# Attention heads' outputs transposed by VectorE in squares of 32 and placed through DRAM; row moments of layers 0 and 2 by ScalarE in two passes

## The reference, cut to what matters

```
h   = layernorm(x)                       # the input of layers 0 and 2
# one layer:
q, k, v = split(shift_token(h) @ wqkv)   # 8 heads of 64
q, k = rotary(l2norm(q)), rotary(l2norm(k))
o   = softmax(q k^T + window mask) v     # windows of 64, looking one window back
x   = h + o @ wo
x   = x + gated MLP(layernorm(shift_token(x)))
```

## Time and profile before

| | us |
|---|---|
| median of 3 runs | 3070.74 (3067.27 to 3071.34) |
| profiled execution | 3069.8 |
| its span, first to last instruction | 3068.0 |
| PE busy | 2989.9 (97%) |
| DVE busy | 2589.6 (84%) |
| ACT busy | 2090.5 (68%) |
| POOL busy | 1746.9 (57%) |

### The profile page before, as it was taken

The page is one execution under the profiler, slowest core; times in us unless marked ns, Lnnn a source line. Parts: engine busy times, 40 slices in busy tenths (PEclk is TensorE's granted clock), DMA queues, the critical chain, the costliest instruction groups (busy, mean ns, idle before and its releaser), DMA issues.

```text
span 3068.0 us, 84550 instructions
## 1 busy us (share of the span) xinstructions
PE 2989.9 (97%) x30773; PEld 2157.2 (70%) x30773; DVE 2589.6 (84%) x5526; ACT 2090.5 (68%) x5016; POOL 1746.9 (57%) x1158
## 2 busy tenths in 40 slices
PE   7999999999999999989999699999999999999999
PEld 4777777667777777657777477777766677777765
DVE  7999998678888888869999599999966888888866
ACT  4777777437777777328889377777753677777732
POOL 8888886125666665540000588888721566666610
PEclk8999999999999999999999799999999999999999
DMA  5222222202222232100000122222320122222221
GB/s 131 50 51 51 50 59 60 48 16 48 49 52 50 51 65 57 41 1 1 1 1 1 24 52 50 53 50 52 70 48 19 42 49 53 50 49 59 57 49 42
DMA packets 311515, 138.26 MB, mean 45 GB/s; under 512 B 225897, under 2 KB 276546, under 8 KB 311106
## 3 DMA queue, kind: packets, MB, share of 16 engines
q1 hardware_dynamic: 311106, 132.84, 19.8%
HBM read 28.13 MB, written 19.66 MB: 16 GB/s over the span
## 4 chain that ended last, share of the span: by engine, by line
PE 90%; DVE 4%; issue 2%; POOL 2%; ACT 1%; SPq 0%; DMA 0%; DVEq 0%; ACTq 0%; POOLq 0%
PE psum L1264 14%; PE psum L1139 11%; PE psum L1238 7%; PE psum L1281 7%; PE psum L1312 7%; PE psum L1292 7%; PE psum L1194 6%; PE psum L1165 5%; PE psum L1226 5%; PE psum L1522 3%; PE psum L1326 3%; PE psum L1339 3%; PE psum L1498 3%; PE psum L1184 3%; PE psum L1508 2%
## 5 line engine op out<-in xcount | busy, mean ns | idle before, releaser
L491 POOL TENSOR_TENSOR rnorm<-ssq_floor,neg_half 128x16 f32<-128x16 f32 x256 | 750.4, 2931 | 499.7 <-DVE qkr L813 494.9
L566 ACT ACTIVATE shared<-psum,neg_max 128x128 f32<-128x128 f32 x2048 | 595.2, 396 | 40.5 <-DVE neg_max L789 40.5
L496 POOL TENSOR_TENSOR qk_cos<-qk_cos,qk_sin 128x1024 f32<-128x1024 f32 x256 | 607.3, 2372 | 0.0
L1264 PE MATMUL psum<-wqkv,hT 128*128 128x512 f32 x1024 | 533.6, 605 | 15.2 <-DVE qk_sin L775 8.5
L587 ACT COPY shared<-psum 128x512 f32<-128x512 f32 x256 | 150.1, 586 | 438.2 <-PE psum L1226 438.2
L775 DVE TENSOR_TENSOR qk_sin<-psum,sin 128x512 f32<-128x512 f32 x512 | 350.5, 685 | 101.8 <-ACT sq L573 100.9
L780 DVE TENSOR_TENSOR qk_cos<-psum,cos 128x512 f32<-128x512 f32 x512 | 350.6, 685 | 80.0 <-ACT sq L573 79.8
L625 ACT ACTIVATE shared<-psum,b1g 128x512 f32<-128x512 f32 (+1 forms) x192 | 131.6, 686 | 353.8 <-PE psum L1139 350.7
L573 ACT ACTIVATE sq<-psum 128x512 f32<-128x512 f32 x512 | 334.2, 653 | 25.3 <-PE psum L1264 25.3
L1139 PE MATMUL psum<-shared,w1g 128*128 128x512 f32 (+1 forms) x768 | 345.6, 593 | 5.4 <-DVE shared L879 4.0
L1292 PEld LDWEIGHTS psum<-wo,shared 128*128 128x128 f32 x2048 | 267.6, 191 | 115.6 <-issue 114.9
(11 more groups left out here) (132 smaller groups left out, 6373.5 us busy)
## 6 DMA issues: line engine op xcount, KB each, us to landing
vprev<-v SPq DMA_DIRECT2D x512, 130.0 KB, 2.3
token_blocks<-blocks SPq DMA_DIRECT2D x236, 64.0 KB, 1.6
hT<-token_blocks SPq DMA_DIRECT2D x944, 16.0 KB, 1.8
shared<-Y SPq DMA_DIRECT2D x32, 256.0 KB
shared<-Y SPq DMA_DIRECT2D x32, 224.0 KB
out<-X SPq DMA_DIRECT2D x8, 512.0 KB, 3.2
X<-in_L_attn_x SPq DMA_DIRECT2D x7, 512.0 KB, 6.7
wqkv<-in_L_ffn_wqkv SPq DMA_DIRECT2D x4, 512.0 KB, 3.6
```

The source lines that it names most:

```text
L491: nc.gpsimd.tensor_tensor(rnorm[:], ssq_floor[:], neg_half[:], ALU.pow).then_inc(rnorm_ready, 1)
L496: nc.gpsimd.tensor_tensor(both, both, qk_sin[:, t.m % 2, :], ALU.add).then_inc(sum_ready, 1)
L566: last = nc.scalar.activation(probs[:, c * P:(c + 1) * P], bank(3 + i, (c % 4) * P, (c % 4 + 1) * P), ACT.Exp, bias=neg_max[:, c:c + 1])
L1264: nc.tensor.matmul(bank(i), hT[:, t.m * P:(t.m + 1) * P], wqkv[:, i * INNER:(i + 1) * INNER], start=True, stop=True).then_inc(qk_psum, 1)
```

## The change

The heads' outputs of tiles 0 to 57 of each layer no longer go through PE. DVE transposes o in place squares of 32 (`heads_blocks`), SP stores the squares to DRAM in 4 DMAs and loads them back transposed in 4 more, and `project_out` reads them. The last 6 tiles keep the old way. DVE's maxima, sums and shares are joined to one instruction each, with the weighted values in PSUM banks 6 and 7 and not 7 and 2. The moments of the pairs of rows in layers 0 and 2 leave DVE: ACT sums a row while copying it (`row_sums`, slot s), POOL makes minus the mean (`row_means`, slot s), ACT sums the squares of row minus mean (`row_squares`, slot s+1), and POOL takes the root and normalises (`normalise_pair`, slot s+1).

```diff
+LAST = 6
...
+        def by_dma(t):
+            return t.row < NT - LAST
+        def act_units(L, s):
+            if L % DEPTH == 0 and s % 2 == 0 and 0 <= s and s + 14 < NT:
+                return range(s + 14, s + 16)
 # SP
+            def store_heads(t):
+                k = dma_count(t)
+                sp.wait_ge(head_blocks_ready, k + 1)
+                wait(sp, heads_in[k % 2], 64 * (k // 2))
+                squares = heads_out[k % 2].rearrange("x i n -> i x n")
+                for b in range(P // SQUARE):
+                    sp.dma_start(squares[:, :, b * SQUARE:(b + 1) * SQUARE],
+                                 head_blocks[b * SQUARE:(b + 1) * SQUARE, k % 2, :]...).then_inc(heads_stored[k % 2], 16)
+            def load_heads(t):
+                sp.wait_ge(heads_stored[k % 2], 64 * (k // 2 + 1))
+                wait(sp, attn_ready, before(t, 2))
+                for j in range(P // SQUARE):
+                    sp.dma_start(o_T[j * SQUARE:(j + 1) * SQUARE, k % 2, :]..., squares[j]).then_inc(heads_in[k % 2], 16)
...
+                if (t := tile_at(L, s - 1)) and by_dma(t):
+                    store_heads(t)
                 if t := tile_at(L, s + 3):
...
+                if (t := tile_at(L, s - 1)) and by_dma(t):
+                    load_heads(t)
 # POOL
+            def row_means(L, s):
+                pool.wait_ge(sum_of_row, p + 1)
...
+                nc.gpsimd.tensor_scalar(row_sum[:, 2:4], row_sum[:, 0:2], -1.0 / P, None,
+                                        ALU.mult).then_inc(mean_of_row, 1)
             def local_slot(L, s):
                 if t := tile_at(L, s + 4):
                     root(t)
                     total(t)
...
+                if act_units(L, s):
+                    row_means(L, s)
+                if rows := act_units(L, s - 1):
+                    normalise_pair(L, s - 1, rows)
 # ACT
+            def row_squares(L, s, rows):
+                act.wait_ge(mean_of_row, p + 1)
+                wait(act, eps_of_row, p)
+                for i, row in enumerate(rows):
+                    last = nc.scalar.activation(Y[:, row, :], X[:, row, :], ACT.Square, bias=row_sum[:, 2 + i:3 + i],
+                                                accum_out=row_sum[:, 4 + i:5 + i])
...
                 if t := tile_at(L, s + 4):
                     squares(t, 1)
+                if rows := act_units(L, s):
+                    row_sums(L, s, rows)
+                if rows := act_units(L, s - 1):
+                    row_squares(L, s - 1, rows)
                 if t := tile_at(L, s):
                     weights(t, 0)
```

More of the change, by code:

```diff
@@ L568, in exponents, with row_sums @@
                 last.then_inc(probs_ready, 1)
+            def row_sums(L, s, rows):
+                if L == 0:
+                    act.wait_ge(loaded[rows[0] // MT], 16)
+                else:
+                    act.wait_ge(x_ready, rows[-1] + 1)
+                wait(act, mean_of_row, pair_count(L, s))
+                for i, row in enumerate(rows):
+                    last = nc.scalar.activation(Y[:, row, :], X[:, row, :], ACT.Copy, accum_out=row_sum[:, i:i + 1])
+                last.then_inc(sum_of_row, 1)
+            def row_squares(L, s, rows):
+                p = pair_count(L, s)
+                act.wait_ge(mean_of_row, p + 1)
+                wait(act, eps_of_row, p)
+                for i, row in enumerate(rows):
+                    last = nc.scalar.activation(Y[:, row, :], X[:, row, :], ACT.Square, bias=row_sum[:, 2 + i:3 + i],
+                                                accum_out=row_sum[:, 4 + i:5 + i])
+                last.then_inc(squares_of_row, 1)
             def squares(t, i):
@@ L584, in outputs @@
             def outputs(t):
-                wait(act, oT_psum, before(t, 0))
+                act.wait_ge(oT_psum, last_count(t) + 1)
                 wait(act, attn_ready, before(t, 1))
@@ L784, in maxima @@
             def maxima(t):
[L785 to L790 removed]
+                scored = psum[:, 3 * BANK:5 * BANK].rearrange("p (h k) -> p h k", k=P)
@@ new lines, in heads_blocks @@
+            def heads_blocks(t):
+                k = dma_count(t)
+                dve.wait_ge(o_ready, t.n + 1)
+                wait(dve, heads_stored[k % 2], 64 * (k // 2))
+                if t.row == 0 and t.L == DEPTH:
+                    dve.wait_ge(out_psum, NT)
+                elif t.row == 0:
+                    wait(dve, mlp_ready, NG * t.L)
+                nc.vector.transpose(head_blocks[:, k % 2, :].rearrange("p (j c n) -> p j c n", j=4, c=4),
+                                    o.rearrange("p (c j n) -> p j c n", c=4, j=4)).then_inc(head_blocks_ready, 1)
@@ L1218, in heads_transpose @@
             def heads_transpose(t):
-                wait(pe, o_ready, before(t, 0, 2))
+                wait(pe, o_ready, before(t, 0))
                 if u := tile_at(t.L, t.row + 3):
@@ L1231, in weigh_values @@
                 pe.wait_ge(vprev_ready[t.m % 4], 32 * (t.n // 4 + 1))
-                wait(pe, o_ready, before(t, 1, 2))
+                wait(pe, o_ready, before(t, 1))
                 pe.wait_ge(probsT_ready, 2 * t.n + 2)
@@ L1272, in project_v @@
                     wait(pe, rot_ready, 4 * (t.n + 1) + 2)
-                elif u := tile_at(t.L, t.row - 5):
-                    wait(pe, oT_ready, before(u, 0))
+                elif u := tile_at(t.L, t.row - 2):
+                    wait(pe, qT_ready, before(u, 0))
                 else:
@@ L1284, in project_out @@
             def project_out(t):
-                wait(pe, oT_ready, before(t, 0))
+                if by_dma(t):
+                    k = dma_count(t)
+                    pe.wait_ge(heads_in[k % 2], 64 * (k // 2 + 1))
+                    squares = o_T[:, k % 2, :].rearrange("p (c n) -> p c n", c=INNER // P)
+                else:
+                    pe.wait_ge(oT_ready, last_count(t) + 1)
                 if t.row == 0:
@@ L1388, in local_slot @@
                     weigh_values(tile(-1))
-                    if t := tile(-2):
-                        heads_transpose(t)
                     if t := tile(4):
```

118 lines of the change are left out of this document (83 added, 35 removed).

## The result

| | before | after |
|---|---|---|
| median, us | 3071.04 (3067.27 to 3073.08, 4 runs) | 3377.37 (3376.26 to 3378.33, 4 runs) |
| profiled execution / its span, us | 3069.8 / 3068.0 | 3378.3 / 3376.3 |
| granted TensorE clock, mean | 0.991 | 0.967 |

The ratio is 1.0999 [1.098, 1.1018]. The direction was predicted, the size not: 3176 was forecast, with a range up to 3280.

The account below looks back on a forecast made before the run. The prediction took PE's own instruction list to bound the kernel, at 8.18 us a slot, with DVE next at 89%. It summed 3069.8 + 158 (mean wait) - 52 (heads' part) = 3176 us, range 3095 to 3280.

Parts of the forecast that it names:

- The wait for the mean: Layers 0 and 2: ACT's `row_squares` waits for POOL's mean; 50 pairs of slots cost 3.15 us more each, +158 us.
- rival B: The mean is there when ACT asks, so all 232 slots gain 0.38 us: 2982 us; chance 0.13.
- The second slot of the pair: Layers 0 and 2: POOL's L491, total and normalisation run 9.3 us without a gap, so POOL sets this slot.
- SP's list: SP's DMA issues and round trip per slot, 8 DMAs added: 7.75 us, hidden behind DVE's 7.8; ends 7.1 and 9.1.
- Rival C: SP bounds too, list 8.5 us, once new DMAs exceed 0.57 each; 136 slots lose 0.34: 3274 us; chance 0.10.
- The last slots of a layer: Late slots with heads by DMA, counted like the others at 7.8 us, a gain of 0.38 each.
- Joined halves and banks: DVE's three joined pairs of operations save 0.07 us each, 0.2 us a slot.
- PE and DVE: Without heads_transpose PE needs 7.69 us a slot; DVE, with a 0.68 us transpose, needs 7.8, against 8.18 before.
- rival E: DVE's 512-element transpose costs 1.2 us, DVE takes 8.3 a slot, the heads' part gains nothing: 3244 us; chance 0.07.
- The sum: Profiled 3069.8 us, plus 158 for 50 pairs, minus 52 for 136 other slots with heads by DMA: 3176 us.

Follow-up runs that it names:

- moments_only: Kernel before with only the moments' part of the change, heads staying on PE: 3253.34 us, 1.0591 to the kernel before.
- squares_later: Kernel after with ACT's `row_squares` of a pair one slot later: 3287.97 us, 1.0704 to the kernel before.
- half_heads: Kernel after with moments back on DVE and heads' outputs by DMA only for every second tile: 3091.61 us, 1.0072 to the kernel before.
- heads_only: Kernel after with the moments back on DVE, leaving the heads' part and joined DVE instructions: 3292.01 us, 1.0716 to the kernel before.
- moments_later: Kernel before with only the moments' part, but `row_squares` one slot later: 3083.03 us, 1.0039 to the kernel before.

## Why the prediction was right and where it failed

- **The wait for the mean** (+158 forecast): the mechanism is right, and the size came out right by luck. 24 pairs in 48 slots of layer 0 gave 74.7 us, where 24 x 3.15 = 75.6 was forecast. At the full granted clock a pair takes 18.96 and would give 24 x 2.63 = 63; the lower clock, a term that the forecast put at nothing without a word, gives the other 12. moments_only shows the wait alone, squares_later takes it away alone. "It would need my placing of tiles to be a slot off", said of rival B, was the right test, and the placing held.
- **The second slot of the pair**, "so POOL sets it": POOL is without idle time in 15 of 24 of these slots in layer 0, as forecast, but with 8.79 and not 9.3 at the full clock. In most of the others, and in most of moments_only, PE's part of the slot runs under the lower clock and POOL waits. The average of 8.97 hides both. "Where a slot had 8.18" is an average too: in layer 0 before, L491 to L491 is 9.32 and 7.04 in turn; the sum over a pair isn't touched by it.
- **SP's list** ("I take 7.75 ... it then hides behind DVE"): this is the step that failed. The list is 7.78 when nothing interferes. But it was compared, as a sum of ordinary durations, with a slot of 7.8, and left no room. In that state each long issue (0.74 us a slot in layer 1) and each late landing (a wait of 0.52 there and not 0.15) lengthens the slot, since nothing on SP absorbs it any more, and the list takes 8.86. The 96 slots of layers 1 and 3 between tiles 4 and 52 were forecast at -0.38 each, -36 us, and came at +68. Rival C had the mechanism with its condition ("as soon as the 8 new DMAs take over 0.57 each") and 8.5 a slot; the DMAs took 0.5 and C came true by another way. C had 0.10, too little, because its chance was tied to one cause.
- **The last slots of a layer**, counted as 7.8: they came at 9.8 and more. `load_tokens` (L440 to L443) puts 4 issues of 0.67 to 0.92 us, 3.1 us together, into two or three of these slots, which then take 12 to 14.5 us. These issues were in the kernel before, and SP had the time for them. The forecast took one ordinary slot for all.
- **Joined halves and banks**, -0.2 us a slot on DVE: this gave nothing, and the turns cost 19 us, 18.6 of them in PE's waits for `shares`. A term of a side edit had been costed only where it runs in the slots.
- **PE and DVE**: the transpose takes DVE 0.711 us, 0.68 was forecast, so rival E's mechanism is out. That the heads' way is sound in itself is shown by layers 1 and 3 of half_heads, where SP has slack. The page "VectorE: DVE Perf Modes" of the Trainium skill, section "Rules for kernel authors", advises TensorE for a transpose of 128x128 where a PSUM destination will do. Its advice held for the kernel as a whole (heads_only is 7% slower), but the runs put the cost in the DMA queue, not in DVE's transpose.
- **The sum** in these terms: pairs +158 and other slots -52 were forecast. Measured are +149 for 48 pairs (126 at the full clock and 23 by the lower one), +68 for 96 slots in layers 1 and 3, +71 for tile 52 to 62 of each layer and +19 for the turns, together 307 of 308.

## What to carry to other kernels

A DMA queue is an engine with a list: add up its issues, the round trips inside it and what one busier slot puts there, and compare with the slot. When the sum is equal to the slot, it is already the bound, because its delays are no longer absorbed. A run with as many DMAs that nobody waits for prices that by itself. Place an instruction that waits for another engine only where the value's whole chain is done by then; here one slot later was worth 89 us with the heads' part and 170 without. Two costs in the same slots don't add, the longer one counts, so a version that undoes one part understates it: heads_only gave back 85 us of moments that cost 182 alone. And where PE stalls in every second slot, look at the granted clock of each slot before calling a right sum right: compare slots at the full clock with each other.

## What the runs showed of the hardware

- Now and then the issue of a DMA takes 1.0 us more than its line's median, once in 21 issues in the kernel after, mostly while a 16 KB packet of instructions is under way or within 0.2 us of one (170 of 186). It follows the DMAs to ACT's queue.
- 64 KB stored in 512 pieces of 128 B land after 2.0 us, 256 KB in 2048 pieces after 3.6; the v copies issued right behind go from 2.4 to 3.6. The page "DMA: Bandwidth & Descriptors" of the Trainium skill, section "Anatomy of one DMA — SWDGE (gpsimd) path", puts a fixed 2.0 us and the bytes at 436 GB/s to a DMA, fitted to DMAs that POOL issues. An estimate by it for 256 KB is 2.6 us; the 3.6 measured for the store here is more.
- The sum along a row on ACT comes as an instruction of its own, 0.19 to 0.28 us, which overlaps the next pass (0.19 at 315.03, the next pass from 315.12): two passes over 128 elements and their sums held ACT for 0.79 us.
- The same 128x128 normalisation on POOL took a mean of 0.64 us (kernel after) and 0.94 (moments_later), so the 1.2 read from one row of before was no constant.
- Where PE waits for the mean in every second slot, the mean granted clock is 0.94 (kernel after, 300 to 400 us), and 1.00 in the same stretch before. It is made of stretches at 0.50, the lower of the two levels (1.2 and 2.4 GHz), during or just behind waits of PE of 2 us and more, and of 1.00 elsewhere. A pair of slots with such a stretch took 19.68 instead of 18.96 in the kernel after, 20.16 instead of 18.83 in moments_only. In moments_later, where the wait is gone, the clock is 1.00 in the same stretch.
